# Routed experts of a decoder: blocks of 128 slots become pairs of half blocks of 64, side by side in PE as column tiles

## The reference

```
score  = sigmoid(h @ Wr)                       # N x 32
chosen = the 8 largest of score + expert_bias  # for each token
share  = score * chosen / sum(score * chosen)
y      = sum over chosen e of share[e] * ((silu(h @ Wg[e]) * (h @ Wu[e])) @ Wd[e])
out    = x + y + (silu(h @ Wsg) * (h @ Wsu)) @ Wsd     # the shared expert
```

## Time and profile before

| what | value |
|---|---|
| median of 3 runs | 2490.97 us (2487.53 to 2496.89) |
| the profiled execution | 2505.32 us |
| its span | 2503.2 us |
| mean granted clock of PE | 0.955 of 2.4 GHz |
| stretch of the 87 blocks | 1099 to 1612.5 us of the span |
| busy in the span | PE 2299.8, PEld 1691.9, DVE 1283.7, ACT 736.1, POOL 859.6 us |

### The profile page before, as it was taken

The page is one execution under the profiler, slowest core; times in us unless marked ns, Lnnn a source line. Parts: engine busy times, 40 slices in busy tenths (PEclk is TensorE's granted clock), DMA queues, the critical chain, the costliest instruction groups (busy, mean ns, idle before and its releaser), DMA issues. The chain is left out here.

```text
span 2503.2 us, 39856 instructions
## 1 busy us (share of the span) xinstructions
PE 2299.8 (92%) x15070; PEld 1691.9 (68%) x15070; DVE 1283.7 (51%) x2314; ACT 736.1 (29%) x1444; POOL 859.6 (34%) x681
## 2 busy tenths in 40 slices
PE   7889999688999998889999999977879999979997
PEld 7658787477888887544444444466657777759997
DVE  4553666547777777442222222276762566653333
ACT  1332222234444443221111111112543323222221
POOL 2333111345556564214444444343433111012220
PEclk9989999798999999989999999988999999969999
DMA  3011000222121210447666879630011000011110
GB/s 120 24 64 55 27 27 2 72 72 72 38 70 37 72 39 1 162 139 187 137 157 168 233 182 270 130 106 24 2 36 75 26 26 26 1 51 51 51 50 30
DMA packets 55203, 194.52 MB, mean 78 GB/s; under 512 B 7524, under 2 KB 7780, under 8 KB 48164
## 3 DMA queue, kind: packets, MB, share of 16 engines
q1 hardware_dynamic: 35540, 145.07, 17.0%
q0 software_dynamic: 19488, 47.05, 9.7%
HBM read 159.20 MB, written 32.90 MB: 77 GB/s over the span
## 5 line engine op out<-in xcount | busy, mean ns | idle before, releaser
L1977 PE MATMUL bank<-m_ring,m_bT 128*128 x696 | 318.0, 600 | 1.5 <-ACT m_bT L1724 0.9
L1977 PEld LDWEIGHTS bank<-m_ring,m_bT 128*128 128x128 f32 x696 | 126.1, 191 | 130.9 <-issue 130.1
L1916 DVE SCALAR_TENSOR_TENSOR m_prod<-bank,m_slot_rows,m_silu 128x256 f32<-128x256 f32 x87 | 42.1, 484 | 285.7 <-ACT m_silu L1711 285.7
L1674 POOL DMA_INDIRECT m_slot_rows<-m_rows,m_idx x87 | 86.2, 991 | 254.1 <-DVE m_prod L1916 213.4
L1711 ACT ACTIVATE m_silu<-bank 128x256 f32<-128x256 f32 (+1 forms) x95 | 36.4, 383 | 449.9 <-PE bank L1977 449.9
L1682 POOL DMA_INDIRECT m_sum<-m_yb,m_idx x87 | 137.9, 1585 | 86.8 <-DVE m_yb L1924 86.8
L1998 PE MATMUL bank<-m_ring,m_aT 128*128 x348 | 163.8, 593 | 1.0 <-DVE m_aT L1930 1.0
L829 ACT ACTIVATE y_att_p_rows<-bank,y_att_n_top 112x375 f32<-112x375 f32 x128 | 71.6, 572 | 189.9 <-DVE y_att_n_top L871 189.9
L220 PE MATMUL bank<-f_hT_hi,f_w_hi 128*128 128x448 f32 x288 | 111.9, 389 | 8.3 <-PEq L86 2.7
L1924 DVE COPY m_yb<-bank 128x512 f32<-128x512 f32 x87 | 60.2, 692 | 101.5 <-PE bank L1998 99.1
L1250 POOL TENSOR_TENSOR f_att_turned<-f_att_turned,consts 128x448 f32<-128x448 f32 x64 | 74.3, 1161 | 101.9 <-ACT f_att_turned L1300 101.9
(11 more groups left out here) (486 smaller groups left out, 5756.4 us busy)
## 6 DMA issues: line engine op xcount, KB each, us to landing
m_ring<-in_m_w SPq DMA_DIRECT2D x32, 1536.0 KB, 7.5
f_raw<-in_f_wq SPq DMA_DIRECT2D x64, 256.0 KB, 2.6
z_raw<-in_z_w SPq DMA_DIRECT2D x7, 1536.0 KB, 6.4
f_att_wo_raw<-in_f_wo SPq DMA_DIRECT2D x16, 512.0 KB, 5.9
x_c_raw<-in_ctxT SPq DMA_DIRECT2D x8, 752.0 KB, 5.5
y_c_raw<-in_ctxT SPq DMA_DIRECT2D x8, 752.0 KB, 4.4
m_sum<-m_slot_rows SPq DMA_DIRECT2D x2, 2048.0 KB, 14.8
a_raw<-in_a_wqk SPq DMA_DIRECT2D x8, 256.0 KB, 3.0
```

Of the source, the lines that this page charges most:

```text
L1674: pool.indirect_dma_start(rows[:, n % 3, :], None, rows_dram[:, :], bass.IndirectOffsetOnAxis(ap=idx[:, n:n + 1], axis=0)).then_inc(rows_i ...
L1977: o = pe.matmul(ps_gu[u % 2][0:m, :], lhs(k), weights(2 * EI * k), start=(k == 0), stop=(k == KC - 1))
```

## The change

The slots are rounded up to half blocks of HP = 64. There are NHALF = 112 + 31 = 143 of them at most, two to a block, so NBLK = 72 blocks; the two halves of a block may belong to different experts. etab and rtab have an entry for each half block. PE does the lower half into partitions 0 to 63 of the bank and the upper half into 64 to 127, as products with 64 stationary columns each; the transposes stay at 128. The lower half reads its weights from the ring, at an address from a register. For the upper half ACT copies the weights out of the ring into the tile upper (two buffers, laid over one_row and one_blk), in three instructions of 128 x 1024 for each block: two for gate and up of block n + 1 ahead of silu n, one for down of n + 1 behind the copy of its rows. DVE's prod takes two instructions, one for each half's share. Each block's scatter becomes two of 64 rows, the lower half always to the first array of sums and the upper half to the second; each waits for the scatter of the block before into the same array. The load of the sums at the end waits for all blocks in both.

```diff
-NBLK = B * S * TOPK // P + E_MOE - 1
+HP = P // 2
+NHALF = B * S * TOPK // HP + E_MOE - 1
+NBLK = (NHALF + 1) // 2
 NBC = NBLK + NBLK % 2
+NHC = 2 * NBC
...
+        upper_at = (nc.sbuf_base + 31) // 32 * 32
         one_row = sb("one_row", [S, 4, TOPK, P], F32R)
         one_blk = sb("one_blk", [S, 4, TOPK, NBC], F32R)
+        assert 4 * TOPK * (P + NBC) >= 2 * EW
+        upper = nc.alloc_sbuf_tensor_at(f"{name}_upper", [P, 2, EW], F32, offset=upper_at)
...
-            for i, into in ((1 - LAST, y), (LAST, x2)):
-                sp.wait_ge(summed[i], 16 * ((NBLK + 1 - i) // 2))
-                if i == LAST:
+            for i, into in ((0, y), (1, x2)):
+                sp.wait_ge(summed[i], 16 * NBLK)
+                if i == 1:
                     sp.wait_ge(x_done, B)
                 for h in range(B // 2):
                     sp.dma_start(into[:, 2 * h:2 * h + 2, :],
                                  sums_dram[i][2 * h * S:2 * (h + 1) * S, :].rearrange("(b s) d -> s b d", b=2)
-                                 ).then_inc(late_in[h] if i == LAST else early_in, 16)
+                                 ).then_inc(late_in[h] if i == 1 else early_in, 16)
...
@@ -1677,10 +1684,14 @@
 
             def scatter(n):
                 pool.wait_ge(yb_done, n + 1)
-                if n >= 2:
-                    pool.wait_ge(summed[n % 2], 16 * (n // 2))
-                pool.indirect_dma_start(sums_dram[n % 2][:, :], bass.IndirectOffsetOnAxis(ap=idx[:, n:n + 1], axis=0),
-                                        yb[:, n % 2, :], None, compute_op=ALU.add).then_inc(summed[n % 2], 16)
+                if n:
+                    pool.wait_ge(summed[0], 16 * n)
+                pool.indirect_dma_start(sums_dram[0][:, :], bass.IndirectOffsetOnAxis(ap=idx[0:HP, n:n + 1], axis=0),
+                                        yb[0:HP, n % 2, :], None, compute_op=ALU.add).then_inc(summed[0], 16)
+                if n:
+                    pool.wait_ge(summed[1], 16 * n)
+                pool.indirect_dma_start(sums_dram[1][:, :], bass.IndirectOffsetOnAxis(ap=upper_idx[:, n:n + 1], axis=0),
+                                        yb[HP:P, n % 2, :], None, compute_op=ALU.add).then_inc(summed[1], 16)
...
+            def upper_slot(n):
+                rank = act.value_load(rtab[0:1, 2 * n + 1:2 * n + 2], min_val=0, max_val=E_MOE - 1)
+                slot = act.snap(rank % RING * EW)
+                act.wait_ge(ring_in, rank * 16 + 16)
+                return slot
+
+            def copy_upper_gate(n, slot):
+                if n >= 2:
+                    act.wait_ge(gu_done, FRONT + n - 1)
+                for i in range(2):
+                    act.activation(upper[:, n % 2, i * KC * EI:(i + 1) * KC * EI], ring[:, bass.ds(slot + i * KC * EI, KC * EI)],
+                                   ACT.Copy).then_inc(upper_done, 1)
+
+            def copy_upper_down(n, slot):
+                if n >= 2:
+                    act.wait_ge(dn_done, FRONT + n - 1)
+                act.activation(upper[:, n % 2, 2 * KC * EI:EW], ring[:, bass.ds(slot + 2 * KC * EI, NC * D)],
+                               ACT.Copy).then_inc(upper_done, 1)
+
             collect_rows(0)
+            act.wait_ge(tabs_done, 4)
+            act.wait_ge(list_done, B)
+            slot = upper_slot(0)
+            copy_upper_gate(0, slot)
+            copy_upper_down(0, slot)
             for n in range(NBLK):
+                if n + 1 < NBLK:
+                    slot = upper_slot(n + 1)
+                    copy_upper_gate(n + 1, slot)
                 silu_of(FRONT + n)
                 if n + 1 < NBLK:
                     collect_rows(n + 1)
+                    copy_upper_down(n + 1, slot)
...
                 dve.tensor_scalar(to_slot[:, :], ps_used[0:1, :], float(EW), None, ALU.mult).then_inc(tab_step, 1)
                 dve.tensor_copy(order[:, :], ps_order[0:1, :]).then_inc(tabs_done, 1)
-                dve.tensor_copy(ends[:, :], ps_ends[0:1, :]).then_inc(tabs_done, 1)
+                dve.tensor_scalar(ends[:, :], ps_ends[0:1, :], 0.5, 0.25, ALU.mult, ALU.add).then_inc(tabs_done, 1)
...
@@ -1868,6 +1907,8 @@
                                   ).then_inc(idx_done, 1)
                 dve.wait_ge(idx_done, 1)
                 dve.scalar_tensor_tensor(idx[:, :], ps_l[:, 0:NBC], -1.0, spare[:, :], ALU.add, ALU.add
+                                         ).then_inc(idx_done, 1)
+                dve.scalar_tensor_tensor(upper_idx[:, :], ps_l[HP:P, 0:NBC], -1.0, spare[HP:P, :], ALU.add, ALU.add
                                          ).then_inc(idx_done, 1)
...
             def prod_block(n):
                 u = FRONT + n
-                expert = dve.value_load(etab[0:1, n:n + 1], min_val=0, max_val=E_MOE - 1)
+                expert = [dve.value_load(etab[0:1, 2 * n + i:2 * n + i + 1], min_val=0, max_val=E_MOE - 1) for i in range(2)]
                 dve.wait_ge(silu_done, u + 1)
                 dve.wait_ge(at_done, u - 1)
-                dve.scalar_tensor_tensor(prod[:, u % 2, :], ps_gu[u % 2][:, EI:2 * EI],
-                                         rows[:, n % 3, bass.ds(expert + D, 1)], silu[:, u % 2, :],
-                                         ALU.mult, ALU.mult).then_inc(prod_done, 1)
+                for i, now in enumerate(halves):
+                    p = dve.scalar_tensor_tensor(prod[now, u % 2, :], ps_gu[u % 2][now, EI:2 * EI],
+                                                 rows[now, n % 3, bass.ds(expert[i] + D, 1)], silu[now, u % 2, :],
+                                                 ALU.mult, ALU.mult)
+                p.then_inc(prod_done, 1)
 
             def collect_y(n):
                 dve.wait_ge(dn_done, FRONT + n + 1)
                 if n >= 2:
-                    dve.wait_ge(summed[n % 2], 16 * (n // 2))
+                    dve.wait_ge(summed[0], 16 * (n - 1))
+                    dve.wait_ge(summed[1], 16 * (n - 1))
                 dve.tensor_copy(yb[:, n % 2, :], ps_d[(FRONT + n) % 2][:, :]).then_inc(yb_done, 1)
...
+            def gate_up(u, b):
                 if u >= 2:
...
+            def gate_up_halves(n, slot):
+                u = FRONT + n
+                pe.wait_ge(prod_done, u - 1)
+                pe.wait_ge(upper_done, 3 * n + 2)
+                for k in range(KC):
+                    at = 2 * EI * k
+                    pe.matmul(ps_gu[u % 2][0:HP, :], bT[:, n % 2, k, 0:HP], ring[:, bass.ds(slot + at, D)],
+                              start=(k == 0), stop=(k == KC - 1))
+                    o = pe.matmul(ps_gu[u % 2][HP:P, :], bT[:, n % 2, k, HP:P], upper[:, n % 2, at:at + D],
+                                  start=(k == 0), stop=(k == KC - 1))
                 o.then_inc(gu_done, 1)
...
-            def down(u, weights):
-                m = P if FRONT <= u < FRONT + NBLK else S
+            def down_waits(u):
                 pe.wait_ge(aT_done, u + 1)
                 if u >= 2:
                     pe.wait_ge(add_done, added_by(u - 2))
                 if u >= FRONT + 2:
                     pe.wait_ge(yb_done, min(u - FRONT - 1, NBLK))
+
+            def down_halves(n, slot):
+                u = FRONT + n
+                down_waits(u)
+                pe.wait_ge(upper_done, 3 * n + 3)
                 for c in range(NC):
-                    o = pe.matmul(ps_d[u % 2][0:m, :], aT[:, u % 2, c, 0:m], weights(2 * KC * EI + c * D),
+                    at = 2 * KC * EI + c * D
+                    pe.matmul(ps_d[u % 2][0:HP, :], aT[:, u % 2, c, 0:HP], ring[:, bass.ds(slot + at, D)],
+                              start=(c == 0), stop=(c == NC - 1))
+                    o = pe.matmul(ps_d[u % 2][HP:P, :], aT[:, u % 2, c, HP:P], upper[:, n % 2, at:at + D],
                                   start=(c == 0), stop=(c == NC - 1))
-                return o.then_inc(dn_done, 1)
-
-            def shared_w(at):
-                return shared[:, at:at + D]
+                o.then_inc(dn_done, 1)
...
             turn_rows(0)
-            slots = []
             for n in range(NBLK):
-                rank_now = pe.value_load(rtab[0:1, n:n + 1], min_val=0, max_val=E_MOE - 1)
+                rank_now = pe.value_load(rtab[0:1, 2 * n:2 * n + 1], min_val=0, max_val=E_MOE - 1)
                 slot = pe.snap(rank_now % RING * EW)
-                slots.append(slot)
                 pe.wait_ge(ring_in, rank_now * 16 + 16)
                 pe.wait_ge(bT_done, n + 1)
-                gate_up(FRONT + n, lambda k: bT[:, n % 2, k, :], lambda at: ring[:, bass.ds(slot + at, D)])
+                gate_up_halves(n, slot)
                 if n + 1 < NBLK:
                     turn_rows(n + 1)
                 if n:
-                    down(FRONT + n - 1, lambda at: ring[:, bass.ds(slots[n - 1] + at, D)])
+                    down_halves(n - 1, slot_before)
                 turn_a(FRONT + n)
-            down(FRONT + NBLK - 1, lambda at: ring[:, bass.ds(slots[NBLK - 1] + at, D)])
+                slot_before = slot
```

(11 more changed lines are left out.)

50 lines of the change are left out of this document (29 added, 21 removed).

## The result

The changed kernel takes 2478.36 us (median of 7 runs, 2468.24 to 2489.46), the kernel before 2493.77 (7 runs, 2487.53 to 2497.90): a ratio of 0.9936, interval 0.9914 to 0.9957. It is 15.4 us faster, where 33.7 had been forecast. The time lies in the range and on the right side; less than half of the gain came.

A forecast was written before the change was run, and what follows sets the result against it. PE's streaming was taken to bound the routed blocks; 41.7 us gained from fewer blocks net of switches, less 3 scatters, 2 start and 3 end, gives 33.7: 2491.0 becomes 2457 us, range 2434 to 2488.

The forecast's parts named there:

- The ring's loads stay 32: Expert weight loads into the ring: their number stays 32, at no cost in the forecast sum.
- 0 within 1 us: Tables growing to 144 columns, lists shrinking to 72, one more index instruction: net cost 0 within 1 us.
- ACT's loop or the scatters setting the pace: Rival for the routed blocks: about 6.8 us a block, 22 us more, 2479 in all; chance 15 in 100.
- landings of 8 us in a row while the ring loads: One condition named for the rival with about 6.8 us a block: scatter landings this slow in succession.
- Scatters: Two half scatters per block, each awaiting the block just before: 3 us taken from a range of 0 to 27.
- Tiles: Block products as two 64-column tiles overlap fully: 12 rounds of 0.43 us as before, weight loads hidden inside the stream.
- Switches: PE enters and leaves column tiles twice per block: 0.64 us a block, bounds 0.36 and 0.8, 46 us in all.
- The base: Block period before the change: 5.854 us, from 503.48 us over 86 periods; PE's streaming sum is 5.81.
- m_prod "costs nothing": DVE's second m_prod instruction per block, 0.48 us, delays the waiting transposes but was claimed to cost nothing.
- a loop, 12.1 us over two blocks: ACT's in-order chain of copies, silu, m_prod and PE's products: 6.0 us per block, below PE's 6.49.
- Copies on ACT: Three weight copies per block at 1.049 us each lie under PE and cost nothing; ACT busy 65%.
- Start and end: Around the blocks: first product 2.6 us later, netted to 2 us; DVE's wait for m_y at the end grows 3.

The follow-up runs named there:

- loads21r5: Changed kernel with only the first 21 of 32 ring loads and a fifth ring slot replacing the spare one; 2457.48 us, 0.9849 of the kernel before.
- regroup_hoist: Changed kernel with each block's tiled products adjacent (two switches), a fourth row buffer, PE's register load ahead of the m_prod wait; 2462.25 us, 0.9867 of the kernel before.
- b_prods: Kernel before with only m_prod split into two instructions of 64 partitions; 2534.71 us, 1.0157 of the kernel before.
- oneprod: Changed kernel with one m_prod of 128 partitions, the two halves' shares first copied into one column; 2478.01 us, 0.9934 of the kernel before.
- full: Changed kernel with one 128-column product instead of two of 64, the upper half getting the lower half's weights; 2476.25 us, 0.9918 of the kernel before.

## Why the prediction was wrong

- **The step that failed** is "The ring's loads stay 32", with "0 within 1 us". The loads themselves are the same; what they wait for is not. Their slots are freed by blocks, and a block now holds two experts. The stall is 14.9 us in the trace, and a fifth slot gives 13.8 us of it back in the time. The rival that came nearest, ACT's loop or the scatters setting the pace, has the right time (2479), but mostly by luck: it puts the cost on every block, and here it lies on two in the middle and on the last ones. The condition that it named for the scatters, landings of 8 us in a row while the ring loads, did come true at the end.
- **Scatters**: 3 us were taken from a range of 0 to 27. 7.1 us come back when the useless loads are gone. They had been priced by their landings in the earlier trace rows, with the maximum of 12.0 in sight; what was missed is that the slow landings are those beside a load of the ring (7.33 us in the median, above the forecast period of 6.49), and that they come in a row at the end, where loads nobody needs run one after another.
- Both together are 20.9 us: `loads21r5` is 38.2 us faster than the kernel before in the same rounds, against 33.7 forecast for the whole.
- **Tiles**: right. Full overlap, 12 rounds of 0.43 (1207.01 to 1207.44 in the trace), and no weight load in the open but the first behind each change of shape. The Trainium skill ("TensorE: Matmul & The Clock Gate", Part 3, The mechanism) has, in its list, a weight load overlap with matmuls in flight only when the row group differs; the same section also lets a load go ahead when it targets the background weight buffer. Two column tiles over the same rows run here in rounds of 0.43 us, as long as those of one full-width product, so the trace differs from the rule in the list, as it did at 32 columns, and does not contradict the other sentence.
- **Switches**: right within 0.04, 0.60 for 0.64. `regroup_hoist` has half of them and a period shorter by 0.30. The rule of the Trainium skill ("TensorEngine Tiling (Array Packing)", Key Properties), that a change of mode drains the engine, fits with this; the trace shows the stop (0.54 us instead of 0.43), not what happens in it.
- **The base** was too high: 5.854 from 503.48/86 took in the odd slow periods; a streaming block is 5.81 (the sum in the prediction's own second paragraph). With 0.60 that is 6.41 and not 6.49, 6 us better over 72 blocks.
- **m_prod "costs nothing"**: right in the number and wrong in the reason. "m_prod ends at 1316.65, they start at 1317.60" was read as slack. It was PE's own issue chain behind the wait; `b_prods` shows every one of the 0.48 us in the open. It was free only because the switches made PE as late. The prediction did sum a loop, 12.1 us over two blocks (its terms add up to 12.0), but not the shorter one over a single block, gate product, silu, m_prod, issue chain, next gate product. Its own terms give 3.48 + 0.51 + 1.01 + 1.17 = 6.17 for that; measured are 6.42.
- **Copies on ACT**: right as to their own time; ACT is busy 280.6 us of 494.5 (57%, 65 forecast). But their place makes the stall longer, which the prediction did not price: ACT wants block 47's weights ahead of silu of block 46. An estimate from the timelines above: the weights were there at about 1406.9, and the gate product of block 47 would have been due at 1391.8 + 6.41 = 1398.2, 8.7 us earlier, against 14.9 measured. No run has the copies elsewhere.
- **Start and end**: from the first gather to the first gate product 11.6 us against 8.2 (3.4 more; 2.6 were forecast, and 2 of them stood in the sum, but the shorter lists gave nothing back: from m_rows<-m_y to the first gather it is 53.1 us in both); from the first shared product behind the blocks to the norm of the next layer 39.8 against 35.1 (4.6 more, 3 forecast), with DVE's wait for m_y at 12.32 us instead of 8.72, as named.
- In the two traces the spans differ by 20.5 us, of which 9.9 lie ahead of the mixture, in stages that are the same in both: m_rows<-m_y starts at 1037.64 in one and 1027.79 in the other (the profiled execution of before was a long one). The mixture itself gives 11.5 in the traces (19.5 from the stretch, less 3.4 and 4.6), the medians 15.4. That the 4 us between them are one execution against seven is argued, not shown.

What stays open: how the small excess of some periods (3.5 us in all in the kernel after, 0.5 in `oneprod`) comes about, though the median times of these two agree.

## What to carry to other kernels

When the unit of work shrinks or comes to hold two owners, look first at buffers whose release is counted in such units: ask how many periods lie between two uses of a slot for the worst neighbours, not on average. A gap between a result and its use can be an engine's own issue chain, and then the whole of any delay ahead of it counts; and where two chains are equally long, test an edit with the other one shortened, or it will look worthless. Transfers whose result nobody reads are not free once something with little slack runs beside them.

## What the runs showed of the hardware that was not expected

A register load and its arithmetic on PE, issued behind a semaphore wait, lie in the open: moving them ahead of the wait took the distance from m_prod's end to the next product from 1.18 to 0.66 us and the kernel `full` from 2476.25 to 2448.46. A scatter of 64 rows holds POOL 1.43 us (lower half) and 1.41 (upper half), one of 128 rows 1.59: half the rows save a tenth of the time. A scatter of 128 rows lands after 4.76 us in the median without a load of the ring beside it, and after 7.33 with one (kernel before). Around PE's idle time of 12.46 us in the stall (1397.9 to 1410.4), its granted clock was 1.00 from 1397 to 1400, 0.50 from 1402 to 1414 and 1.00 again from 1415, so PE's first 4 us of work ran at half speed.
